# Sums of squares as streaming products in column tiles, and a recurrence in 32x32 tiles, on one core

## What is computed

```python
def _l2norm(x, eps=1e-06):
    return x * lax.rsqrt(jnp.sum(x * x, axis=-1, keepdims=True) + eps)
q = _l2norm(q)
k = _l2norm(k)
```

```python
def step(s, inp):
    q_, w_, k_, v_, a_, b_ = inp
    sa = jnp.einsum('bhij,bhj->bhi', s, a_)
    s = s * w_[:, :, None, :] + sa[..., None] * b_[:, :, None, :] + v_[..., None] * k_[:, :, None, :]
    return (s, jnp.einsum('bhij,bhj->bhi', s, q_))
_, y = jax.lax.scan(step, s0, (qt, wt, kt, vt, at, bt))
y = ((yg - mu) / jnp.sqrt(var + EPS)).reshape(Bx, Tx, C) * ln_w + ln_b
y = y + (rk * v.reshape(Bx, Tx, H, HS)).reshape(Bx, Tx, C)
return y * g @ Wo.T
```

## Time and profile before

| | |
|---|---|
| median of 3 runs | 5312.93 us (5308.17 to 5330.14) |
| profiled execution | 5314.12 us, span 5312.3 us |
| PE, DVE, ACT, POOL busy | 4563.9, 3708.1, 2767.1, 2332.2 us |
| instructions | 119470 |
| mean granted PE clock | 0.872 |

### The profile page before, as it was taken

How to read it: one execution, slowest core, us unless ns; L and a number is a source line. 1 busy time by engine, 2 the same in 40 slices (tenths; PEclk the granted TensorE clock), 3 DMA queues, 4 the chain that set the end, 5 groups by cost and what they waited for, 6 DMA issues and landing times. The chain is left out here.

```text
span 5312.3 us, 119470 instructions
## 1 busy us (share of the span) xinstructions
PE 4563.9 (86%) x44570; PEld 3259.9 (61%) x44570; DVE 3708.1 (70%) x8727; ACT 2767.1 (52%) x6775; POOL 2332.2 (44%) x1892
## 2 busy tenths in 40 slices
PE   5888988999898898989799899964588788998998
PEld 3676776777676767776666466531356665655665
DVE  5666667767766777666588488556799547866874
ACT  2554545555555555544588388534200117865882
POOL 2444434444444444444476177224322126734751
PEclk7888879888887898888799899977799659998998
DMA  2000000000000000000000000000000000000000
GB/s 87 8 9 10 8 8 10 8 8 10 10 9 7 10 10 8 8 10 10 31 0 0 29 1 0 1 7 0 8 1 1 1 31 1 0 25 5 0 0 16
DMA packets 170138, 53.43 MB, mean 10 GB/s; under 512 B 142304, under 2 KB 166112, under 8 KB 168928
## 3 DMA queue, kind: packets, MB, share of 16 engines
q1 hardware_dynamic: 168160, 44.20, 3.8%
q10 hardware_dynamic: 1536, 3.21, 0.2%
HBM read 36.89 MB, written 10.49 MB: 9 GB/s over the span
## 5 line engine op out<-in xcount | busy, mean ns | idle before, releaser
L865 DVE SCALAR_TENSOR_TENSOR gd_qkT<-gd_ps,gd_w_qk,gd_qkT 128x256 f32<-128x256 f32 x768 | 367.1, 482 | 193.0 <-ACT gd_qkT L683 172.3
L430 PE MATMUL gd_ps<-gd_taps,gd_xwins 128*128 128x512 f32 x1024 | 464.8, 597 | 0.0
L1624 ACT ACTIVATE L_ffn_s<-L_ffn_s,L_ffn_nb,L_ffn_r 128x128 f32<-128x128 f32 x1024 | 419.5, 482 | 3.2
L1062 POOL TENSOR_TENSOR gd_gV<-gd_g,cst 128x512 f32<-128x512 f32 x128 | 130.4, 1042 | 621.6 <-ACT gd_X L742 621.6
L1444 POOL TENSOR_TENSOR L_ffn_t<-L_ffn_t 128x512 f32<-128x512 f32 x128 | 190.3, 1486 | 396.6 <-DVE L_ffn_t L1665 396.6
L430 PEld LDWEIGHTS gd_ps<-gd_taps,gd_xwins 128*128 128x128 f32 x1024 | 192.4, 191 | 190.9 <-issue 185.4
L1663 DVE TENSOR_TENSOR L_ffn_t<-L_ffn_ps,L_ffn_sb_rope 128x512 f32<-128x512 f32 x256 | 176.7, 690 | 101.8 <-PE L_ffn_ps L1469 101.8
L1113 POOL TENSOR_TENSOR gd_gate<-gd_gate,gd_o 128x512 f32<-128x512 f32 x128 | 159.5, 1281 | 153.3 <-DVE gd_o L959 153.3
L1512 PEld LDWEIGHTS L_ffn_ps<-L_ffn_kT,L_ffn_qT 64*64 64x64 f32 (+1 forms) x4096 | 148.5, 137 | 114.2 <-issue 98.7
L1446 POOL TENSOR_TENSOR L_ffn_r<-L_ffn_ss,L_ffn_mhalf 128x8 f32<-128x8 f32 x128 | 211.0, 1648 | 10.4 <-DVE L_ffn_ss L1687 5.2
L1453 POOL TENSOR_TENSOR L_ffn_r<-L_ffn_ss,L_ffn_mhalf 128x8 f32<-128x8 f32 x128 | 211.3, 1651 | 0.0
(11 more groups left out here) (403 smaller groups left out, 13787.9 us busy)
## 6 DMA issues: line engine op xcount, KB each, us to landing
L_ffn_sb_rope<-in_rope SPq DMA_DIRECT2D x4, 2048.0 KB, 8.4
gd_tap_row<-in_L_attn_conv_v SPq DMA_DIRECT2D x2, 2048.0 KB, 15.8
gd_blocks<-gd_nA SPq DMA_DIRECT2D x256, 16.0 KB, 1.7
gd_Z<-gd_blocks SPq DMA_DIRECT2D x32, 128.0 KB, 2.0
gd_inverses<-gd_Z SPq DMA_DIRECT2D x32, 128.0 KB, 1.7
gd_gV<-gd_inverses SPq DMA_DIRECT2D x256, 16.0 KB, 1.9
L_ffn_sb_wqkv<-in_L_ffn_wqkv SPq DMA_DIRECT2D x4, 768.0 KB, 9.3
out<-out_tok SPq DMA_DIRECT2D x8, 256.0 KB, 2.7
```

Source lines behind the costliest of these rows:

```text
L430: ins = pe.matmul(ps[4 + i % 2][:], xwin(j)[:, t:t + P], taps[:, t, 512 * i:512 * (i + 1)], start=(t == 0), stop=(t == TAPS - 1))
L865: ins = dve.scalar_tensor_tensor(produced(j, i), ps[6 + i % 2][:, P + t:P + t + WIDE], w_tap[:, at, t:t + 1], produced(j, i), ALU.mult, AL ...
L1624: ins = act.activation(s[b][:, i, k], s[b][:, i, k], ACT.Exp, scale=r[b][:, h:h + 1], bias=nb[b][:, i, k:k + 1])
```

## The change

In the first mixer the sums of squares change sides: the indicator columns (now two tables of 32 columns) are the weights and the squares stream through, 256 columns at a time, in four column tiles that accumulate over two pairs. ACT copies the sums, PE turns them to tokens by two transposes, and DVE reads the turned sums. In the second mixer's outputs, DVE makes chunk matrices of 32 x 32 blocks with its own 32 x 32 transpose, all ahead of use; a state step is an identity product and four 32 x 32 products per batch; POOL spreads half blocks, the outputs are made in pieces of two chunks, and the order on PE and ACT is one loop over steps with the offsets in `AT_*`. DVE's order is written anew.

```diff
-C_END = C_HALVES + 2
+C_END = C_HALVES + 2 * 32
-    t[:, C_HALVES:C_HALVES + 2] = i[:, None] // HALF == np.arange(2)[None, :]
+    for x in range(2):
+        for y in range(2):
+            t[:, C_HALVES + 32 * x + 2 * x + y] = i // HALF == y
...
-        SUMS = slice(448, 480)
+        SUMS = slice(WIDE, 2 * WIDE)
...
-                def square_sums(turn, q):
-                    w(sq_s.now(turn, q))
-                    for i in (2 * q, 2 * q + 1):
-                        for c in range(2):
-                            at = SUMS.start + 2 * PAIRS * c + 2 * i
-                            ins = pe.matmul(ps[6][:, at:at + 2], qk_sq[:, i, P * c:P * (c + 1)], cst[:, C_HALVES:C_HALVES + 2], start=True, stop=True)
-                    if q == 3:
-                        ins.then_inc(ss_mm.sem, 1)
+                def square_sums(turn):
+                    for i in range(PAIRS):
+                        if i % 2 == 0:
+                            w(sq_s.now(turn, i // 2))
+                        x, z = divmod(i, 4)
+                        ins = pe.matmul(ps[6][32 * z:32 * (z + 1), 0:WIDE], cst[:, C_HALVES + 32 * x:C_HALVES + 32 * (x + 1)], qk_sq[:, i], start=(x == 0), stop=(x == 1))
+                    ins.then_inc(ss_mm.sem, 1)
+
+                def turn_square_sums(turn):
+                    w(sbh_s.now(turn))
+                    for c in range(2):
+                        ins = pe.transpose(ps[6][:, SUMS.start + P * c:SUMS.start + P * (c + 1)], sums_by_head[:, P * c:P * (c + 1)], ident)
+                    ins.then_inc(ss_mm.sem, 1)
...
                     turn_k(n, j)
-                    for i in range(4):
-                        if follows:
-                            square_sums(n + 1, i)
-                        project_gate(n, j, i)
+                    if follows:
+                        square_sums(n + 1)
+                    project_gate(n, j, 0)
+                    project_gate(n, j, 1)
+                    if follows:
+                        turn_square_sums(n + 1)
+                    project_gate(n, j, 2)
+                    project_gate(n, j, 3)
...
+                def copy_square_sums(turn):
+                    w(ss_mm.now(turn, 0))
+                    act.activation(sums_by_head[:], ps[6][:, 0:WIDE], ACT.Copy).then_inc(sbh_s.sem, 1)
...
                     token_major_k(n)
+                    if follows:
+                        copy_square_sums(n + 1)
                     for i in range(4):
                         silu_gate(n, i)
...
+SUB = 32
+AT_Y, AT_SQUARE, AT_ROOT, AT_TURN, AT_OUT = (9, 13), (22, 28), (25, 32), (28, 35), (32, 41)
...
+                def turned_M(k, b):
                     n = nth(k, b)
+                    src = S[:, b, RS:2 * RS, chunks(k)].rearrange("p j c -> p c j").unsqueeze(2).to_broadcast([P, BLK, SUB // RS, RS])
+                    mask = head4[:].unsqueeze(1).unsqueeze(3).to_broadcast([P, BLK, SUB // RS, RS])
+                    if k:
+                        dve.wait_ge(t_s, nth(k - 1, b) + 1)
+                    dve.tensor_tensor(Ms[b][:].rearrange("p c (h j) -> p c h j", j=RS), src, mask, ALU.mult).then_inc(m_s, 1)
+                    dve.wait_ge(m_s, n + 1)
+                    dve.transpose(MT[:, b, chunks(k)].rearrange("p c i -> p (c i)"), Ms[b][:].rearrange("p c j -> p (c j)")).then_inc(t_s, 1)
...
+                for k in range(NBLK):
+                    for b in range(B):
+                        turned_M(k, b)
+                for k in range(NBLK):
+                    centred(k, 0)
+                    if k:
+                        gated(k - 1, 1)
+                    sums(k, 0)
+                    scaled(k, 0)
+                    centred(k, 1)
+                    if k:
+                        residual(k - 1, 1)
+                    gated(k, 0)
+                    sums(k, 1)
+                    scaled(k, 1)
+                    residual(k, 0)
+                gated(NBLK - 1, 1)
+                residual(NBLK - 1, 1)
...
                     pe.matmul(out, ident, S[:, :, 0:RS, c], start=True, stop=False)
-                    pe.wait_ge(ev_s, 8 * k + 2 * (j // 4) + 2)
+                    if c % BLK == 0:
+                        pe.wait_ge(t_s, nth(c // BLK, 1) + 1)
...
                     for b in range(B):
-                        ins = pe.matmul(out[:, b], MT[k % 2][:, b, j], S0[:, c, b], start=False, stop=(b == B - 1))
+                        for r in range(P // SUB):
+                            ins = pe.matmul(out[quad(r), b], MT[quad(r), b, c], S0[quad(r), c, b], start=False, stop=(b == B - 1))
                     ins.then_inc(st_mm, 1)
...
-                    for i in range(BLK // QUARTERS):
-                        j = BLK // QUARTERS * q + i
-                        out = ps_y[b][CS * i:CS * (i + 1), P * q:P * (q + 1)]
+                    for i in range(2):
+                        j = half * (u % 2) + 2 * piece + i
+                        q, at = j // 4, j % 4
+                        out = ps_y[b][CS * at:CS * (at + 1), P * q:P * (q + 1)]
...
+                for s in range(PACE):
+                    if s < CB - 1:
+                        advance(s)
+                    for b in range(B):
+                        u, piece = divmod(s - AT_Y[b], half)
+                        if 0 <= u < 2 * NBLK and piece < 4:
+                            corrected(u, b, piece)
+                    for b in range(B):
+                        k, at = divmod(s - AT_TURN[b], BLK)
+                        if at == 0 and 0 <= k < NBLK:
+                            turn_back(k, b)
+                        k, at = divmod(s - AT_OUT[b], BLK)
+                        if at == 0 and 0 <= k < NBLK:
+                            project(k, b)
```

More of the change, by code:

```diff
@@ L659, in _ @@
                 w(conv_s.now(0))
-                for i in range(4):
-                    square_sums(0, i)
+                square_sums(0)
+                turn_square_sums(0)
                 w(ss_s.now(0))
@@ L804, in _ @@
                 silu(0, -2, PAIRS - 1)
+                copy_square_sums(0)
                 exp_ab(1)
@@ L874, in square_sums @@
                     w(ss_mm.now(turn))
-                    sums = ps[6][:, SUMS].rearrange("p (c k two) -> p c two k", two=2, k=4)
-                    by_head = lambda t: t[:].rearrange("p c h -> p (c h)").rearrange("p (c two k) -> p c two k", two=2, k=4)
+                    sums = ps[6][:, SUMS].rearrange("p (c z g) -> p c g z", c=2, z=4)[:, :, 0:4]
+                    by_head = lambda t: t[:].rearrange("p c (g z) -> p c g z", z=4)
                     if j % 2 == 0:
@@ L2403, in sb @@
             return ctx.enter_context(nc.sbuf_tensor("wo_" + name, shape, F32))
-        M = sb("M", [P, B, BLK, RH, RS])
+        MT = sb("MT", [P, B, CB, SUB])
+        Ms = [sb(f"Ms{b}", [P, BLK, SUB]) for b in range(B)]
         S0 = sb("S0", [P, CB, B, RS])
@@ L2591, in _ @@
                 act.wait_ge(zero, 2)
-                for g in range(8):
-                    turned(0, g)
-                for k in range(NBLK + 2):
-                    for j in range(BLK):
-                        if BLK * k + j < CB - 1:
-                            state(BLK * k + j)
-                        if k + 1 < NBLK and j % 2 == 1:
-                            turned(k + 1, j // 2)
-                        if j in (9, 13):
-                            squares(k - 1, j // 13)
-                        if j in (10, 14):
-                            root(k - 1, j // 14)
+                act.activation(warm[:], eps[:], ACT.Sqrt, bias=eps[:], scale=1.0 / RS)
+                for s in range(PACE):
+                    if s < CB - 1:
+                        state(s)
+                    for b in range(B):
+                        k, at = divmod(s - AT_SQUARE[b], BLK)
+                        if at == 0 and 0 <= k < NBLK:
+                            squares(k, b)
+                        k, at = divmod(s - AT_ROOT[b], BLK)
+                        if at == 0 and 0 <= k < NBLK:
+                            root(k, b)
             @block.gpsimd
@@ L2607, in _ @@
                 pool.wait_ge(zero, 2)
-                for k in range(NBLK):
-                    pool.wait_ge(st_s, min(BLK * k + BLK - 1, CB - 1))
+                for u in range(2 * NBLK):
+                    at = slice(half * (u % 2), half * (u % 2 + 1))
+                    pool.wait_ge(st_s, half * u + half - 1)
                     for b in range(B):
-                        if k:
-                            pool.wait_ge(yc_mm, QUARTERS * (nth(k - 1, b) + 1))
-                        src = S0[:, chunks(k), b].unsqueeze(2).to_broadcast([P, BLK, RH, RS])
-                        mask = head.unsqueeze(1).unsqueeze(3).to_broadcast([P, BLK, RH, RS])
-                        pool.tensor_tensor(S0x[b][:], src, mask, ALU.mult).then_inc(x_s, 1)
+                        if u >= 2:
+                            pool.wait_ge(yc_mm[b], QUARTERS * (u // 2 - 1) + 2 * (u % 2 + 1))
```

(3 more changed lines are left out.)

116 lines of the change are left out of this document (29 added, 87 removed).

## The result

The changed kernel takes **5152.27 us** (median of 4 runs, 5149.41 to 5160.31), the kernel before 5310.55 (5303.66 to 5330.14): ratio 0.9693, 95% interval 0.9672 to 0.9715, 158 us less where 68 were forecast.

| from the first to the last instruction | before | after | gain | forecast |
|---|---|---|---|---|
| first mixer | 2535.0 | 2472.9 | 62.1 | 30 |
| second mixer's outputs | 205.8 | 118.1 | 87.7 | 38.4 |
| all the rest of the span | | | 4.1 | 0 |

The account below looks back on a forecast made before the run. PE was taken to bound the first mixer's even chunks, the inverse chain the odd ones. Gains of 30 + 8.9 + 25.5 + 4 = 68.4 us gave 5314.1 - 68.4 - 1.2 = 5244 us, range 5215 to 5272.

Parts of the forecast that it names:

- the three half-clock stretches: First mixer, three even chunks at half clock: they stay, and the new square sums save 3.5 us in each.
- the price of a state step and its piece: Second mixer's outputs at half clock: identity product 0.61, four-tile passes 0.45, piece 1.10, together 2.16 us.
- upper bound (3 x 10): First mixer: three half-clock stretches of some 21 us each vanish, with half of their time gained.
- The 12 other even chunks: First mixer at full clock: 1.7 us less PE time in each, less 1 for the tight one.
- The odd chunks: First mixer: PE only comes earlier to a DMA wait that exists already, so the gain is 0.
- The outputs, start: Second mixer's outputs: smaller spreads bring the first state step after 3.9 us instead of 12.7, gaining 8.9 us.
- The outputs, steps: Second mixer's outputs: all state steps with pieces take 136 us instead of 161.5, gaining 25.5 us.
- rival 2: Outputs get the full clock: a step takes about 1.3 us, 50 us less, total 5194 us; chance 0.12.
- The outputs, end: Tail of the outputs: only half a block of POOL's last spreads is left, gaining 4 us (0 to 8).
- 1: Rival: the inverse chain takes all of the first mixer's gain, total 5274 us; chance 0.12.
- 3: Rival, outputs: a state step's four tiles go one after another, 1.05 instead of 0.45 us, total 5282 us; chance 0.05.
- 4: Rival, first mixer: longer DMA waits in odd chunks cost the clock, 160 us slower, total 5404 us; chance 0.05.

Follow-up runs that it names:

- e3: Kernel before, with its four groups of two-column square sums put together ahead of the first gate product: 5352.82 us, ratio 1.0064.
- e10: Changed kernel with four idle two-column products (eight passes) put back ahead of each gate product: 5218.04 us, ratio 0.9835.
- e2: Kernel before with only the outputs' part of the change: 5240.95 us, ratio 0.9845, runs in two groups.
- e5: Changed kernel with four unused 512-column products in a row ahead of the outputs' first piece: 5147.81 us, ratio 0.9677; run again, 5141.76 us.
- e6: Kernel before with four unused 512-column products in a row ahead of the first output product of its block 1: 5309.70 us, ratio 0.9982.
- e7: Changed kernel with four unused 512-column products in a row, and outputs in four-chunk pieces every second step: 5156.80 us, ratio 0.9690.
- e4: Changed kernel with one unused 512-column product in each of the two steps where the outputs' first pieces begin: 5181.94 us, ratio 0.9735.
- e12: Changed kernel, nothing altered, repeated on the same chip as a run with four added products: 5150.06 us, ratio 0.9688.
- e9: Changed kernel, nothing altered, repeated for its spread: 5152.92 us (5145.96 to 5171.05), ratio 0.9696.

## Why the prediction was wrong

**The step that failed is the clock**, in both stages. In the first mixer "the three half-clock stretches" were taken to stay, with 3.5 us less each, and the outputs were costed at 0.50 from end to end. The runs show other levels: full clock for most of those stretches, and for the outputs from 4140 to the last state step. Of the 85.5 us by which the profiled span's gain exceeds the forecast (153.9 for 68.4), the clock makes some 46: 18 in the first mixer and 28 in the outputs. A second step failed beside it, the price of a state step and its piece, which makes 16; the rest is in the smaller terms below. With the clock as forecast the kernel would, by this estimate, still have come out near 5198 us (5152 + 46), under the range, so the clock alone does not explain the miss.

*First mixer, 62.1 for 30.* From one chunk's first L582 product (L591 after) to the next, the chunks 4, 8 and 20 went from 88.9, 89.3 and 85.9 us to 78.8, 79.1 and 78.1: 28.2 us where 10.5 were counted. The prediction had this as its upper bound (3 x 10) and took the low value. In all nine profiles with the new form the stretches are short, and e3 and e10 tell in part why: thin products alone can bring the clock down, and put back between the gates they lengthened one of the three stretches again. The 12 other even chunks gave 23.6 us (forecast 20.4 less 1), though seven of them now wait for the DMA. The sums cost 1.22 us there, not 1.54: the 16 passes take 1.00, not 1.10, and the 0.22 counted for the changed shape doesn't show beside it. The odd chunks gave 7.2 for a forecast 0, and the first and last 4.5; the tail of the last chunk took 1.4 back. For these small terms only the trace speaks, no run, and their cause stays open. PE's waits for nothing shown ahead of the solve's second product went down to 46.5 us from this in the kernel before:

```profile
PE gd_ps L518 <- issue: 53.8, 36, 2.5
```

The inverse chain may also start earlier with the sums.

*The outputs, start.* 12.7 to 3.75 us, 9.0 for 8.9: right.

*The outputs, steps.* 70.4 us for 25.5, in two parts. At 0.50 the whole run of steps takes 119 us (e2), not 136: the identity product and the four-tile passes take 0.86 us together, not 1.06, and a piece 1.02, not 1.10. That is 53 x 0.27 + 10 x 0.20 = 16 us. The prediction's 0.61 us for the identity product was the length of its row, which the next row overlaps; from start to start it is 0.53. The other 28 (119 to 91) are the clock, from 4140 on. This is rival 2, put at 0.12 and 50 us. It named the right mechanism and, as its reason against, narrower products; what the runs show instead is that a piece in every step kept the full clock and output products in half of the steps did not (e5 against e6 and e7).

*The outputs, end.* 31.5 to 23.3 us, 8 for 4, the end of the given bound. The clock is not the reason: in e2, at 0.50 to the last state step, the end took 24.3 us.

*The rivals.* 1 came true in part: its sign, DMA waits in even chunks, appeared in seven of them and the waits rose by 18 us, but the chain took only a part of the gain. 3 fell: the 16 passes of four row tiles into one bank take 0.33 us, less than the 0.45 taken and far from the 1.05 of one tile after another. The prediction cites the Trainium skill for this rival, TensorEngine Tiling (Array Packing), "Gotcha 1: PSUM Pressure": row tiles cannot access one bank at the same time. The trace does not agree: the rule cost nothing here. 4 fell: the odd chunks had 19.2 us each at 0.50 before and 19.9 after. Its price was read from the chunk at 433 us as what follows "an idle gap of 2.38 us", but the clock fell there at 430.8, only 0.4 us into that gap.

With rival 2 in full and the three stretches at their upper bound (another 20 us) the prediction's own figures give 5244 - 50 - 20 = 5174 us, 22 above the time. The two were weighed each by itself; that both are the same thing, PE's clock after a change of its work, was missed. The range's upper end does not follow from its terms: 25 us of the step bound and 15 of the first mixer above 5244 give 5284, not 5272. It bears on nothing here, for the time lies under the lower end.

## What to carry to other kernels

Cost a stretch that lies at half clock twice, at either level, and ask what its mix of products will be after the change, not only how many there are: a stretch in which PE is busy throughout can lie at half clock. When a step is priced from a timeline, take the time from start to start, not the length of a row. Where steps must be thin, dense work in every step may keep the clock where the same work in every second step does not (e5, e7). A few dense products at the head, whose result is not used, may pay: here 6.3 us of them gave 8 us and a steady time. Where a kernel's runs stand in groups, compare the clock of one stage before explaining the median.

## What the runs showed of the hardware

- PE was busy for all of a stretch and the clock was at 0.50 throughout: 115 us in e2, 81 us in e7.
- Thirty-two two-column passes in a row (3.98 us, e3) brought the clock from 1.00 to 0.50 with no idle time; eight at a time between gate products at 1.00 did not the earlier trace rows.
- Two single products of 2.08 us with thin steps and a piece between them raised nothing (e4, profiled execution). With four in a row, 6.33 us, the clock rose within them (e5, and in e6 and e7 too).
- One stage of the same program took 118.1 us where the clock rose 51 us after its start (e12) and 129.1 where it rose 79 us after (e9); the executions of e2 stood in two groups 39 us apart.
- Sixteen passes of 32 x 32 tiles on four row groups, into one PSUM bank, took 0.33 us from start to start at 0.50.
